# A masked attention layer on one core: seven instead of eight blocks of a tile transposed by DMA, and a row bias raised by a constant

## The reference

```python
h = jnp.maximum(_layernorm(x, axis=-1), 0.0)             # x: 8192 x 128
scores = jnp.einsum('nd,md->nm', h, ks)                  # ks: 8192 x 128
scores = jax.nn.leaky_relu(scores, negative_slope=0.2)
scores = jnp.where(adj > 0, scores, -9000000000000000.0) # adj: 8192 x 8192 int32
attn = jax.nn.softmax(scores, axis=1)
out = x + jnp.einsum('nm,md->nd', attn, ks)
```

## Time and profile before

| | |
|---|---|
| median of 3 runs | 1802.88 us (1799.99 to 1807.59) |
| the profiled execution, its own time | 1804.0 us |
| its span | 1802.2 us |
| busy: PE, PEld, DVE, ACT, POOL | 90%, 66%, 87%, 89%, 42% |
| granted TensorE clock | 0.994 of full speed |
| DMA | 421.91 MB, mean 234 GB/s, mean busy share of the 16 engines 98% |

### The profile page before, as it was taken

The page is one execution under the profiler, slowest core; times in us unless marked ns, Lnnn a source line. Parts: engine busy times, 40 slices in busy tenths (PEclk is TensorE's granted clock), DMA queues, the critical chain, the costliest instruction groups (busy, mean ns, idle before and its releaser), DMA issues. The chain is left out here.

```text
span 1802.2 us, 37484 instructions
## 1 busy us (share of the span) xinstructions
PE 1617.3 (90%) x13442; PEld 1185.6 (66%) x13442; DVE 1564.4 (87%) x2592; ACT 1606.0 (89%) x2081; POOL 750.0 (42%) x713
## 2 busy tenths in 40 slices
PE   5799898898898898898898998988988988989988
PEld 3466666676666676666676666666766666666666
DVE  7888898898888888888888888988988888888885
ACT  7798898898898898898898988988988988989988
POOL 1344344443443443443443443444434434434433
PEclk9899999999999999999999999999999999999999
DMA  7699999999999999999999999999999999999996
GB/s 216 189 241 232 243 237 242 244 230 242 240 237 239 238 241 235 245 239 234 245 232 242 241 234 243 234 237 250 231 242 245 227 245 238 221 246 242 234 246 125
DMA packets 613686, 421.91 MB, mean 234 GB/s; under 512 B 547968, under 2 KB 580736, under 8 KB 580736
## 3 DMA queue, kind: packets, MB, share of 16 engines
q1 hardware_dynamic: 613504, 419.53, 97.7%
HBM read 281.02 MB, written 4.19 MB: 158 GB/s over the span
## 5 line engine op out<-in xcount | busy, mean ns | idle before, releaser
L322 POOL TENSOR_TENSOR halves<-scores,halves 128x512 f16<-128x512 f32 x512 | 596.5, 1165 | 995.0 <-ACT halves L485 995.0
L607 DVE CUSTOM_DVE_ANT_0 scores<-ps_scores,mask,minus_scale 128x1024 f32<-128x1024 f32 x512 | 654.8, 1279 | 3.3 <-PE ps_scores L370 2.7
L468 ACT ACTIVATE scores<-scores,neg_max 128x1024 f32<-128x1024 f32 x512 | 582.3, 1137 | 0.0
L461 ACT ACTIVATE scores<-scores 128x1024 f32<-128x1024 f32 x512 | 537.6, 1050 | 9.8 <-DVE pair_min L607 9.7
L368 PE MATMUL ps_scores<-keysT_hi,hT_hi 128*128 128x512 f16 x1024 | 390.2, 381 | 166.3 <-DVE hT_lo L536 154.1
L616 DVE TENSOR_TENSOR probsT_lo<-ps_T,probsT_hi 128x512 f16<-128x512 f32 x512 | 351.8, 687 | 192.2 <-ACT probsT_hi L476 192.0
L476 ACT ACTIVATE probsT_hi<-ps_T 128x512 f16<-128x512 f32 x512 | 305.6, 597 | 167.5 <-PE ps_T L379 161.9
L394 PE MATMUL ps_out<-keys,probsT_hi 128*128 128x258 f16 x2048 | 399.6, 274 | 6.3 <-issue 4.5
L370 PE MATMUL ps_scores<-keysT_hi,hT_lo 128*128 128x512 f16 x1024 | 390.4, 381 | 0.0
L589 DVE TENSOR_SCALAR mask<-adj_in 128x2048 bf16<-128x2048 int32 x256 | 390.1, 1524 | 0.1
L369 PE MATMUL ps_scores<-keysT_lo,hT_hi 128*128 128x512 f16 x1024 | 390.0, 381 | 0.0
(11 more groups left out here) (52 smaller groups left out, 749.1 us busy)
## 6 DMA issues: line engine op xcount, KB each, us to landing
adj_in<-in_adj_dram SPq DMA_DIRECT2D x256, 1024.0 KB, 5.6
turned<-halves SPq DMA_TRANSPOSE x512, 6.0
x_in<-in_x_dram SPq DMA_DIRECT2D x64, 64.0 KB, 5.3
keys_in<-in_L_gnn_ks_dram SPq DMA_DIRECT2D x8, 512.0 KB, 7.3
x_res<-in_x_dram SPq DMA_DIRECT2D x64, 64.0 KB, 4.9
out_dram<-out_tile SPq DMA_DIRECT2D x64, 64.0 KB, 5.3
```

Of the source, the lines that this page charges most:

```text
L322: nc.gpsimd.tensor_tensor(half[:, BLOCK:2 * BLOCK], probs(t, b), half[:, 0:BLOCK], ALU.subtract) \
L461: nc.scalar.activation(s, s, ACT.Prelu, alpha=1.0 / SLOPE).then_inc(leaky_ready, 1)
L468: nc.scalar.activation(s, s, ACT.Exp, bias=neg_max[:, t % 2:t % 2 + 1], scale=-SLOPE) \
L607: nc.vector.tensor_tensor_reduce(out=score_pair(q, p), in0=ps_scores[:, slots, :].rearrange("p s k -> p (s k)"), in1=mask[:, (p // 2) % 2, ...
```

## The change

Block 15 moves from `BY_DMA` to `BY_PE`: seven blocks (1, 3, ... 13) are transposed by DMA and nine by TensorE. With its lags, its transpose, high half and low half fall in sub-step j = 3 of the next step, its output in j = 5 (it was j = 9). The bias is raised by the constant 7.99 where it was raised by 14 ln 2 if a test of its size allowed it; `lift`, its instruction and its semaphore go. The means to put some high halves on VectorE, of which nothing was in use, go as well. Line numbers of the changed kernel are lower by 16 on TensorE, ScalarE and in `split_probs_lo`.

```diff
-    BY_DMA = tuple(b for b in range(BLOCKS) if b % 2 == 1)
+    BY_DMA = tuple(b for b in range(BLOCKS) if b % 2 == 1 and b != 15)
     BY_PE = tuple(b for b in range(BLOCKS) if b not in BY_DMA)
-    HI_ON_DVE = tuple(b for b in BY_DMA if False)
-    HI_ON_ACT = tuple(b for b in BY_DMA if b not in HI_ON_DVE)
...
-    LIFT = 14 * 0.6931471805599453
-    LIFT_BELOW = 2.0 ** 22
+    LIFT = 7.99
...
-                if b in HI_ON_DVE:
-                    pool.wait_ge(half_hi_dve_ready, nth_dve(t, b) + 1)
-                else:
-                    pool.wait_ge(half_hi_ready, nth_act(t, b) + 1)
+                pool.wait_ge(half_hi_ready, n + 1)
...
-                    split = behind(i, j, HI_LAG, HI_ON_ACT, this, prev)
+                    split = behind(i, j, HI_LAG, BY_DMA, this, prev)
...
                 dve.wait_ge(plain_max_ready, q + 1)
-                nc.vector.tensor_scalar(lift[:, :], plain_max[:, :], plain_max[:, 0:1], LIFT_BELOW ** 2,
-                                        ALU.mult, ALU.is_lt) \
-                    .then_inc(lift_ready, 1)
-                dve.wait_ge(lift_ready, q + 1)
                 if q > 1:
                     dve.wait_ge(probs_ready, (q - 1) * PAIRS)
-                nc.vector.scalar_tensor_tensor(out=neg_max[:, q % 2:q % 2 + 1], in0=lift[:, :], scalar=LIFT,
-                                               in1=plain_max[:, :], op0=ALU.mult, op1=ALU.add) \
+                nc.vector.tensor_scalar(neg_max[:, q % 2:q % 2 + 1], plain_max[:, :], LIFT, None, ALU.add) \
                     .then_inc(neg_max_ready, 1)
```

More of the change, by code:

```diff
@@ L38, in gat_kernel @@
     HI_LAG = 2
-    HI_DVE_LAG = 3
     LO_LAG = 3
@@ L109, in gat_kernel @@
         plain_max = sbuf("plain_max", [P, 1], fp32)
-        lift = sbuf("lift", [P, 1], fp32)
         neg_max = sbuf("neg_max", [P, 2], fp32)
@@ L152, in gat_kernel @@
         plain_max_ready = sem("plain_max_ready")
-        lift_ready = sem("lift_ready")
         neg_max_ready = sem("neg_max_ready")
@@ L161, in gat_kernel @@
         half_hi_ready = sem("half_hi_ready")
-        half_hi_dve_ready = sem("half_hi_dve_ready")
         half_lo_ready = sem("half_lo_ready")
@@ L190, in nth_pe @@
             return t * len(BY_PE) + sum(c < b for c in BY_PE)
[L192 to L196, removed]
         def nth_dma(t, b):
@@ L617, in split_probs_lo @@
                                         ALU.subtract).then_inc(T_lo_ready, 1)
[L619 to L625, removed]
             def minimum(q):
@@ L689, in step @@
                         split_probs_lo(*split)
-                    split = behind(i, j, HI_DVE_LAG, HI_ON_DVE, this, prev)
-                    if split:
-                        split_half_hi(*split)
                     if ahead:
```

## The result

The changed kernel takes 1881.82 us (median, 1881.67 to 1883.28), the kernel before 1804.49 beside it. The ratio is 1.0432, 95% interval 1.0408 to 1.0457: slower by 77 us, where 45 were forecast, and above the range. The profiled execution has a span of 1880.0 us, 77.8 more than before, and a mean granted TensorE clock of 0.972 where it was 0.994.

What follows compares the result with a forecast made beforehand. TensorE back to back plus a chain through VectorE was taken to bound a step. 62 steps at +0.74 us (45.9), less small gains, gave +45 us: 1848 us, 2.5% slower, range 1814 to 1862.

Steps and rivals of the forecast that it cites:

- TensorE's gap: TensorE's wait before a step's first score, for the low half of h: expected to grow from 2.4 to 2.7 us.
- Undisturbed step: From one first score to the next: predicted to grow by 0.74 us, from 27.30 to 28.04, in 62 steps.
- Transposes +0.44: Block 15's four transposes on TensorE at j = 3 add 0.44 us in each of 62 steps, with no idle to hide it.
- `lift` -0.19: In the chain at the step's end, removing `lift` gains a net 0.19 us a step, all on the path.
- Hand-over to ScalarE: The lead passes from TensorE to ScalarE: block 10's copy 0.78 us late, the last `add_mask` 0.69 late instead of 0.44.
- too little slack (0.08 a pair): ScalarE's round takes 3.00 us of a 3.08 us pair, so lateness early in a step is paid back at 0.08 a pair.
- GpSimd's hold of `plain_max`: At the step's end, `plain_max` is held until GpSimd's low half of block 13 is done, lasting about 0.7 us.
- VectorE's extra low half at j = 3: Block 15's low half, 0.60 us on VectorE behind pair 1's `add_mask`, fits where VectorE had waited for ScalarE.
- TensorE keeping the lead (1818): Rival: ScalarE or VectorE has more slack, so the step grows by only 0.25 us, giving 1818 us; chance 0.11.
- No catching up (1861): Rival: ScalarE stays 1.12 us late to the step's end, so the step grows by 0.93, giving 1861 us; chance 0.08.
- DMA as the bound: Rival: transposes by DMA set the pace, so one fewer saves 68 us and the kernel takes 1735 us; chance 0.04.
- the share of 1.01: DMA engines shown busy at 1.01 of the stretch; read as counting packets in flight rather than a full engine.

Runs made afterwards that it cites:

- e3: Changed kernel with 24 matmuls, into PSUM columns nothing reads, behind TensorE's last output of a step to fill its gap: 1842.0 us, ratio 1.0198.
- e4: Changed kernel with block 15's output back at j = 9 and six slots for transposed halves instead of three: 1823.8 us, ratio 1.0098.
- e1: Kernel before with only the new bias (`lift` gone, constant 7.99), eight blocks still by DMA: ratio 0.9974.
- e7: Changed kernel with `plain_max` made by `tensor_scalar` from one full input instead of the instruction with two inputs: 1817.8 us, ratio 1.0073.
- e2: Kernel before with only block 15 moved from DMA to TensorE, `lift` kept: 1913 us, ratio 1.0591.
- e6: Kernel before with the new bias and the halves of h made before the last pair's `add_mask`, eight blocks by DMA: 1659.9 us, ratio 0.9191.
- e8: Kernel before with `lift` computed one extra time and waited for, lengthening the gap: 1838.9 us.
- e9: Kernel before with `lift` computed two extra times, each waited for, lengthening the gap: 1896.3 us.

## Why the prediction was wrong

**The step that failed is the assumption that TensorE's clock stays up.** The prediction read a clock of 1.00 for a stretch of the kernel before, and took every duration from there. It had TensorE's gap nearly right (2.7 us expected, 2.55 found: the step is 0.07 shorter, and TensorE's own work in it grew by 0.52, not 0.44), and put no price on it. 23 long steps at 1.67 us are 38 us; the kernel before has one, 1.6 us. With 60 x 0.67 = 40 us for the undisturbed step, this makes 77 of the 77.8 us of the spans. e3, where only the gap is filled, takes 40 us off the kernel, and no step is long.

The kernel before already had such a step, in the trace that the prediction was made from: one of 28.95 us that begins behind a longer gap than usual, with a mean clock of 0.94.

```profile
1529.01 0.39 PE L368 MATMUL ps_scores<-keysT_hi,hT_hi 128*128 128x512 f16 x1 [2.77 <-DVE hT_lo L536]
```

```profile
1529.01:1557.96 28.95, 26.55 (x210) 19.21 (x210) 24.00 (x41) 24.68 (x32) 11.69 (x11) 0.94 1.00 228
```

So a price of 1.65 us and a gap of the length that was forecast stood there to be read. How often the clock would fall could not be read from one case.

**Undisturbed step, +0.74 forecast, +0.67 found.** Right in its parts, but for one size. Transposes +0.44: shown by e4, 27.49 - 27.30 + 0.25. `lift` -0.19: it was 0.25 (e1), mostly since `hT_hi` follows `neg_max` by 0.09, not 0.13. This was the only mis-sized term. One sum slips by 0.02: 870.29 + 0.97 for block 13's half is 871.26, not 871.24, so the forecast's own terms give +0.76. Hand-over to ScalarE: right to 0.04 us at block 10, and e4 shows that the moved output is its cause. That the delay then lasts because ScalarE has too little slack (0.08 a pair) was read and not tried apart; the unled copies 3.00, 2.98 and 2.99 apart agree with it. GpSimd's hold of `plain_max`: forecast at 0.7, found 0.77, and shown by e7.

**VectorE's extra low half at j = 3** cost nothing that can be seen, as forecast: its copy is on time, and the `add_mask` of the last pair starts at 877.84, for 877.88 forecast. In e4, which has the low half too, the step grows by no more than the transposes.

**The rivals.** TensorE keeping the lead (1818) fell with the unled copies. No catching up (1861) fell likewise. DMA as the bound fell: no gain came from a block less by DMA, neither in e2 nor where e6's DMA is busiest. What the prediction says of the share of 1.01, that it counts packets in flight, does not stand in the Trainium skill; it is the prediction's own reading, and the traces bear it out: a share can pass 1.00 only where packets overlap, and in e6 it is 1.13. None had the clock. That was the fault in the set of rivals, more than the weights: a rival "the gap grows, and the clock falls after it" could have been priced from the step at 1529.01.

## What to carry to other kernels

A gap of TensorE has two prices: its own length, and the chance that the clock falls in the work behind it. In this kernel the second was up to 54 us in 1913. A mean clock of 0.97 hints at it, and single steps show it: look at the distribution of step lengths. So before making a chain shorter by a tenth, ask whether it must lie on the path at all; here, cutting one instruction out was worth 0.3%, and with two small instructions moved ahead of what they don't depend on as well, 8%. When a block of work is moved between engines, count where its later stages land in the order: here their place cost 0.48 us a step, as much as the work itself (0.44).

## What was not expected of the hardware

- The clock fell with gaps as short as 2.00 us (4 steps of e7; its fifth had a gap of 2.36) and stayed up in the kernel before after every gap of 2.40 us from its fourth step on. Filling a gap of 2.55 us down to 1.21, or one of 2.15 down to 0.82, with matmuls kept it up in all of 60 steps.
- Where it falls in relation to the gap differs. In the changed kernel it is 0.7 to 1.4 us into the new work, at 1.6 to 1.7 us each time. In e1 it is within 0.15 us of the first score. In two falls of e8 and eight of e9 it is inside the gap; these cost 1.3 us in e8 and 2.8 to 2.9 in e9.
- A `tensor_scalar` of one column took 0.21 us as `lift` and 0.15 as `neg_max`. The first takes its scalar from a tensor, the second as a constant; this was only seen, not tried. e7's `plain_max`, with a scalar from a tensor, took 0.21 as well.
